# Cross-attention with experts on Trainium2: weighted sums of two steps made together, x transposed in one piece

## The reference

```python
def _L0_xattn_ref(x, y, Wq, Wkv, Wproj, bproj):
    q = (x @ Wq).reshape(b, lq, H, DK).transpose(0, 2, 1, 3)
    kv = (y @ Wkv).reshape(b, lkv, 2, H, DK).transpose(2, 0, 3, 1, 4)
    k, v = (kv[0], kv[1])
    atten = softmax(einsum('bhid,bhjd->bhij', q, k) * SCALE, axis=-1)
    res = einsum('bhij,bhjd->bhid', atten, v)
    return res.transpose(0, 2, 1, 3).reshape(b, lq, H * DK) @ Wproj + bproj
...
x = x + _L0_xattn_ref(_layernorm(x), ctx_768, Wq, Wkv, Wproj, bproj)
x = x + _L0_ffn_ref(_layernorm(x), gate_w, gate_up_w, down_w)   # top 2 of 8 experts, silu(gate) * up, down
```

## Time and profile before

| | |
|---|---|
| median of 3 runs | 1473.92 us (1473.84 to 1474.1) |
| the profiled execution | 1469.35 us, of which the span of the profile is 1467.6 |
| PE busy | 1426.4 us (97% of the span) |
| DVE busy | 1054.7 us (72%) |
| ACT busy | 854.5 us (58%) |
| POOL busy | 624.9 us (43%) |
| PE's granted clock | 0.994 of full speed over the span |
| the chain that ended last | PE 91%, DVE 3%, DMA 3% |
| W blocks in that chain (L1555) | 11%; transposes of exponentials (L1531) 10% |

### The profile page before, as it was taken

One profiled execution on the slowest core, in us unless ns is written; L12 is line 12 of the kernel. 1 busy time (PEld: TensorE's weight loads), 2 busy tenths in 40 slices (PEclk: granted clock), 3 DMA queues, 4 the chain that ended last, 5 costly groups with the idle time before them and its releaser, 6 DMA issues.

```text
span 1467.6 us, 38599 instructions
## 1 busy us (share of the span) xinstructions
PE 1426.4 (97%) x11960; PEld 1264.4 (86%) x11961; DVE 1054.7 (72%) x2868; ACT 854.5 (58%) x2392; POOL 624.9 (43%) x671
## 2 busy tenths in 40 slices
PE   6999999999999999999999999999997999999996
PEld 5888889888888888888888898888886788888885
DVE  5667777777777777777777777777767776666664
ACT  5566556555665566656655656566555565555553
POOL 3634344344545343544344444545436243333332
PEclk9999999999999999999999999999999999999999
DMA  9322222222222232322222222212128243333232
GB/s 264 108 68 69 75 72 76 67 76 67 73 67 75 72 88 76 99 74 67 73 67 77 70 73 70 73 38 73 31 64 312 50 69 54 57 51 57 51 57 26
DMA packets 101508, 114.75 MB, mean 78 GB/s; under 512 B 17276, under 2 KB 88172, under 8 KB 101356
## 3 DMA queue, kind: packets, MB, share of 16 engines
q1 hardware_dynamic: 88300, 95.25, 22.3%
q0 software_dynamic: 12144, 15.66, 6.0%
q10 hardware_dynamic: 1024, 3.34, 0.7%
HBM read 62.28 MB, written 51.93 MB: 78 GB/s over the span
## 4 chain that ended last, share of the span: by engine, by line
PE 91%; DVE 3%; DMA 3%; issue 1%; ACT 0%; ACTq 0%; POOLq 0%; DVEq 0%; SPq 0%
PE bank L1486 26%; PE bank L1429 21%; PE bank L1555 11%; PE bank L1531 10%; PE bank L1521 9%; PE bank L1576 6%; PE bank L1493 4%; DMA out<-y_out,dest_now 2%; PE bank L1729 2%; DVE probT L1285 1%; PE bank L1682 1%; DVE Wgu L1138 1%; DMA WkU_whole<-in_L_xattn_Wkv 1%; DVE stat L1127 0%; DVE x L1125 0%
## 5 line engine op out<-in xcount | busy, mean ns | idle before, releaser
L891 ACT ACTIVATE prob<-bank,neg_max 112x375 f32<-112x375 f32 x512 | 300.4, 589 | 136.1 <-DVE neg_max L1279 136.1
L1279 DVE TENSOR_REDUCE neg_max<-bank 112x1 f32<-112x375 f32 x512 | 243.8, 539 | 16.4 <-PE bank L1521 16.3
L1531 PE MATMUL bank<-ident,prob 112*125 112x112 f32 x1536 | 213.8, 273 | 2.6 <-ACT prob L891 2.4
L1531 PEld LDWEIGHTS bank<-ident,prob 112*125 112x125 f32 x1536 | 198.3, 188 | 16.1 <-ACT prob L891 4.7
L1555 PEld LDWEIGHTS bank<-probT,V 125*64 125x64 f32 x3072 | 149.0, 137 | 39.7 <-issue 37.0
L822 POOL DMA_INDIRECT out<-y_out,dest_now x63 | 97.8, 1552 | 199.9 <-DMA out<-y_out,dest_now 139.8
L1046 DVE TENSOR_TENSOR K_l<-bank,K_h 128x376 fp32r<-128x376 f32 x256 | 140.3, 549 | 57.1 <-ACT K_h L847 52.7
L1555 PE MATMUL bank<-probT,V 125*64 125x112 f32 x3072 | 176.6, 264 | 3.3 <-DVE probT L1285 2.5
L1429 PE MATMUL bank<-Wgu,hT_h 128*128 x504 | 164.7, 408 | 3.4 <-DVE hT_l L1347 2.8
L845 ACT COPY V<-bank 125x512 f32<-125x512 f32 x96 | 56.4, 587 | 164.7 <-PE bank L1493 162.2
L847 ACT CAST K_h<-bank 128x376 fp32r<-128x376 f32 x256 | 121.0, 473 | 31.2 <-PE bank L1486 29.7
(11 more groups left out here) (217 smaller groups left out, 3962.1 us busy)
## 6 DMA issues: line engine op xcount, KB each, us to landing
bins<-pad_rows SPq DMA_DIRECT2D x29, 1032.0 KB, 6.0
inv_rows<-sums SPq DMA_DIRECT2D x126, 128.0 KB, 2.9
h_in<-bins SPq DMA_DIRECT2D x63, 129.0 KB, 2.2
Wgu<-in_L_ffn_gate_up_w SPq DMA_DIRECT2D x6, 1024.0 KB, 6.8
y_sb<-in_ctx SPq DMA_DIRECT2D x32, 187.5 KB, 2.7
y_sb<-in_ctx SPq DMA_DIRECT2D x62, 93.8 KB, 2.7
x_sb<-in_x SPq DMA_DIRECT2D x16, 224.0 KB, 2.9
x_res<-in_x SPq DMA_DIRECT2D x32, 112.0 KB, 2.5
```

The lines of the kernel that those rows point to most:

```text
L891: nc.scalar.activation(prob[:, j, :], S_ps[j][0:LQ, 0:LKV], ACT.Exp, bias=neg_max[:, j:j + 1], accum_out=row_sum[:, head // HB, head % HB: ...
L1279: nc.vector.tensor_reduce(neg_max[:, j:j + 1], S_ps[j][0:LQ, 0:LKV], AX.X, ALU.max, negate=True).then_inc(max_done, 1)
L1531: last = nc.tensor.transpose(S_ps[j][0:KR, t * LQ:t * LQ + LQ], prob[:, j, t * KR:t * KR + KR], ident[0:LQ, 0:LQ])
```

## The change

The weighted sums of steps 0 and 1 are made together at the end of step 1, those of steps 2 and 3 at the end of step 3, in all pairs but the last (`merged`). For that `probT` becomes two buffers, one for even and one for odd steps. Scores of odd steps now wait for the copies of the even step's turned exponentials themselves, since `weigh` no longer stands in between. The K, V and q products stay in their steps. The four transposes of x are one item, "early" in step 3 of the even batch; q 7 moves from "mid" to "late" in step 2 of the even batch. ACT's and DVE's copies of x's transposes are one of 448 columns in place of two of 224.

The second `probT` takes the place of tables of the experts, which move to the region of `Wd`. So the first part of `Wd` is loaded not at the start of pair 14 but in the even batch of pair 15, behind the first expert's weights, and SP waits there until the weighted sums of all earlier pairs are made.

```diff
--- before.py
+++ after.py
@@ -71,12 +71,12 @@
 
 
     q_at = {(1, 0): (0,), (1, 1): (1,), (1, 2): (2, 3), (1, 3): (4,), (0, 0): (5,), (0, 1): (6,), (0, 2): (7,)}.get((odd, s), ())
-    one = [("q", p) for p in q_at] + {(0, 2): [("xT", 0)], (0, 3): [("xT", 1)]}.get((odd, s), [])
+    one = [("q", p) for p in q_at] + {(0, 3): [("xT", 0)]}.get((odd, s), [])
     places = {"K": [("K", 2 * s), ("K", 2 * s + 1)],
               "early": one if s != 2 else [],
-              "mid": one[:1] if s == 2 else [],
+              "mid": one[:-1] if s == 2 else [],
               "V": [("V", t) for t in {0: ((1, 1), (1, 2)), 1: ((0, 0), (0, 1)), 3: ((0, 2), (1, 0))}.get(s, ())],
-              "late": one[1:] if s == 2 else []}
+              "late": one[-1:] if s == 2 else []}
     return [(odd, s, place, kind, a) for place in PLACES for kind, a in places[place]]
 
 
@@ -84,7 +84,7 @@
 SECOND = ((1, 2), (0, 1), (1, 0))
 PAIR = [it for odd in (0, 1) for s in range(NS) for it in ahead(odd, s)]
 START = [(1, -1, "K", kind, a) for kind, a in (
-    ("K", 0), ("xT", 0), ("xT", 1), ("K", 1), ("K", 2), ("K", 3), ("q", 0), ("q", 1), ("K", 4), ("K", 5), ("q", 2),
+    ("K", 0), ("xT", 0), ("K", 1), ("K", 2), ("K", 3), ("q", 0), ("q", 1), ("K", 4), ("K", 5), ("q", 2),
     ("K", 6), ("K", 7), ("q", 3), ("q", 4), ("V", (0, 0)), ("V", (0, 1)), ("V", (0, 2)), ("V", (1, 0)))]
 START_BANKS = [k % 6 for k in range(len(START) - 4)] + [6, 7, 0, 1]
 LAST = [it for it in PAIR if it[3] != "xT" and not (it[0] and (it[3] in "Kq" or it[4] not in NOW))]
@@ -197,6 +197,11 @@
 def by_vector(b):
 
     return not known(b) or b < B - 3
+
+
+def merged(i):
+
+    return not known(i) or i < NP - 1
 
 
 def dram_at(t, b):
@@ -250,11 +255,7 @@
         place["at"] += 2 * 2 * 2 * FF * 4
         shared_from = place["at"]
         gw_wide = nc.alloc_sbuf_tensor_at("gw_wide", [LQ, E, C], F32, offset=wgu_at)
-        gw_rows = nc.alloc_sbuf_tensor_at("gw_rows", [LQ, C, E], F32, offset=wgu_at + E * C * 4)
-        weighed = nc.alloc_sbuf_tensor_at("weighed", [LQ, 2, C], F32, offset=wgu_at + E * C * 4)
-        multiplied = nc.alloc_sbuf_tensor_at("multiplied", [LQ, E // 2, C], F32, offset=wgu_at + E * C * 4 + 2 * C * 4)
-        logits = nc.alloc_sbuf_tensor_at("logits", [LQ, E], F32, offset=wgu_at + E * C * 4 + (2 + E // 2) * C * 4)
-        assert 2 * E * C * 4 <= shared_from - wgu_at
+        assert E * C * 4 + 4 * KT * LQ * 4 <= shared_from - wgu_at
 
 
         WqH = sb("WqH", [P, 2, HD], F32R)
@@ -269,7 +270,8 @@
         q_l = sb("q_l", [P, NJ, 2 * LQ], F32R)
         V = sb("V", [KR, KT, HD], F32)
         prob = sb("prob", [LQ, 4, LKV], F32)
-        probT = sb("probT", [KR, 4, KT * LQ], F32)
+        probT = [sb("probT", [KR, 4, KT * LQ], F32),
+                 nc.alloc_sbuf_tensor_at("probT_odd", [KR, 4, KT * LQ], F32, offset=wgu_at + E * C * 4)]
         x_sb = sb("x_sb", [LQ, 2, C], F32)
 
 
@@ -328,6 +330,12 @@
         wd_at = base + size - E * FJ * C * 4
         assert place["at"] <= wd_at
         early = 2
+        gw_rows = nc.alloc_sbuf_tensor_at("gw_rows", [LQ, C, E], F32, offset=wd_at)
+        place["at"] = wd_at
+        weighed = sb("weighed", [LQ, 2, C], F32)
+        multiplied = sb("multiplied", [LQ, E // 2, C], F32)
+        logits = sb("logits", [LQ, E], F32)
+        assert place["at"] <= wd_at + early * FJ * C * 4 and E <= early * FJ
         place["at"] = wd_at + early * FJ * C * 4
         y_sb = sb("y_sb", [P, 2, 2, LKV], F32)
         yA_h = sb("yA_h", [P, 2, LKE], F32R)
@@ -532,9 +540,6 @@
 
             def pair(i):
                 a = Ahead(i)
-                if known(i) and i == NP - 2:
-                    sp.dma_start(Wd[:, 0:early].rearrange("p e k n -> p (e k) n"),
-                                 down_w[0:early].rearrange("e (k p) n -> p (e k) n", p=P)).then_inc(wd_early, 16)
                 for odd in (0, 1):
                     b = 2 * i + odd
                     if there(b, B):
@@ -555,7 +560,10 @@
                         spread_inverses(b, 0)
                     if known(i) and i == NP - 1 and not odd:
                         sp.wait_ge(gates_done, B - 3)
+                        sp.wait_ge(pv_made, NS * (B - 2))
                         load_expert(sp, 0)
+                        sp.dma_start(Wd[:, 0:early].rearrange("p e k n -> p (e k) n"),
+                                     down_w[0:early].rearrange("e (k p) n -> p (e k) n", p=P)).then_inc(wd_early, 16)
                     if known(i) and i == NP - 1 and odd:
                         sp.dma_start(Wd[:, early:E].rearrange("p e k n -> p (e k) n"),
                                      down_w[early:E].rearrange("e (k p) n -> p (e k) n", p=P)).then_inc(wd_in, 16)
@@ -665,7 +673,7 @@
                 pool.tensor_tensor(std1[:, :, 1], std1[:, :, 0], minus_half[:, 0:2], ALU.pow).then_inc(rs1, 1)
                 if not known(pair) or pair > 0:
                     a = Ahead(pair - 2 if not known(pair) or pair > 1 else None)
-                    pool.wait_ge(made, a.made(a.find(int(a.first), "xT", 1)))
+                    pool.wait_ge(made, a.made(a.find(int(a.first), "xT", 0)))
                 pool.wait_ge(rs1, pair + 1)
                 pool.sem_inc(passed, 1)
                 for r in range(2):
@@ -848,8 +856,7 @@
                 elif kind == "q":
                     nc.scalar.copy(q_h[:, arg, :], src[:, 0:2 * LQ]).then_inc(hi_done, 1)
                 else:
-                    nc.scalar.copy(xT_h[:, :, arg * LQ:arg * LQ + LQ],
-                                   src[:, 0:2 * LQ].rearrange("p (k q) -> p k q", k=2)).then_inc(hi_done, 1)
+                    nc.scalar.copy(xT_h[:].rearrange("p k q -> p (k q)"), src[:, 0:4 * LQ]).then_inc(hi_done, 1)
 
             def hi_of_experts(first, end):
                 for e in range(first, end):
@@ -891,10 +898,10 @@
                 nc.scalar.activation(prob[:, j, :], S_ps[j][0:LQ, 0:LKV], ACT.Exp, bias=neg_max[:, j:j + 1],
                                      accum_out=row_sum[:, head // HB, head % HB:head % HB + 1]).then_inc(exp_done, 1)
 
-            def turned(b, s, j):
+            def turned(b, s, j, to):
 
                 act.wait_ge(probT_made, H * b + 4 * s + j + 1)
-                nc.scalar.copy(probT[:, j, :], S_ps[j][0:KR, 0:KT * LQ]).then_inc(probT_second, 1)
+                nc.scalar.copy(to[:, j, :], S_ps[j][0:KR, 0:KT * LQ]).then_inc(probT_second, 1)
 
             def sum_experts(b):
 
@@ -940,8 +947,9 @@
                         if s == 1 and there(b - 2, B):
                             open_gates(b - 2, logits if by_vector(b - 2) else C_ps)
                         if there(b, B):
-                            turned(b, s, 2)
-                            turned(b, s, 3)
+                            to = probT[s % 2 if merged(i) else 0]
+                            turned(b, s, 2, to)
+                            turned(b, s, 3, to)
                         if s == 0 and there(b - 2, B) and by_vector(b - 2):
                             sum_experts(b - 2)
                         for k in made_at["late"]:
@@ -1041,8 +1049,8 @@
                 elif kind == "q":
                     lo, ps, hi = q_l[:, arg, :], src[:, 0:2 * LQ], q_h[:, arg, :]
                 else:
-                    lo, hi = xT_l[:, :, arg * LQ:arg * LQ + LQ], xT_h[:, :, arg * LQ:arg * LQ + LQ]
-                    ps = src[:, 0:2 * LQ].rearrange("p (k q) -> p k q", k=2)
+                    lo, hi = [t[:].rearrange("p k q -> p (k q)") for t in (xT_l, xT_h)]
+                    ps = src[:, 0:4 * LQ]
                 nc.vector.tensor_tensor(lo, ps, hi.bitcast(F32), ALU.subtract).then_inc(lo_done, 1)
 
 
@@ -1279,10 +1287,10 @@
                 nc.vector.tensor_reduce(neg_max[:, j:j + 1], S_ps[j][0:LQ, 0:LKV],
                                         AX.X, ALU.max, negate=True).then_inc(max_done, 1)
 
-            def turned(b, s, j):
+            def turned(b, s, j, to):
 
                 dve.wait_ge(probT_made, H * b + 4 * s + j + 1)
-                nc.vector.tensor_copy(probT[:, j, :], S_ps[j][0:KR, 0:KT * LQ]).then_inc(probT_first, 1)
+                nc.vector.tensor_copy(to[:, j, :], S_ps[j][0:KR, 0:KT * LQ]).then_inc(probT_first, 1)
 
             def pair(i):
                 a = Ahead(i) if there(i, NP) else None
@@ -1304,12 +1312,13 @@
                             normalise(b, 0)
                         if s == 2 and there(b - 1, B):
                             residual(i, b - 1, 1 - odd, A_ps[1])
+                        to = probT[s % 2 if merged(i) else 0]
                         if there(b, B):
-                            turned(b, s, 0)
+                            turned(b, s, 0, to)
                         for k in made_at["early"]:
                             low_part(a, k)
                         if there(b, B):
-                            turned(b, s, 1)
+                            turned(b, s, 1, to)
                         for k in made_at["mid"]:
                             low_part(a, k)
```

(24 more changed lines are left out.)

## The result

The changed kernel takes 1497.8 us (median of 6 runs, 1495.98 to 1500.69) where the kernel before takes 1474.01 (6 runs beside it, 1472.93 to 1476.83). The ratio is 1.016, with a 95% interval of 1.0149 to 1.0172: slower by 1.6%. The forecast was 1493, slower. The profiled execution took 1498.88 us, its span 1497.1. That is 29.5 more than the span before, 6 more than the medians differ. Some 2.9 of it is the load at the start: the first scores stand at 33.74 for 30.81, and this start lay anywhere from 29.8 to 33.7 in the profiles of this study. The rest is the loop: 14 pairs at 70.96 for 69.03 are 27.0.

A forecast was written before the change was run, and what follows sets the result against it. PE, busy 199.86 of 200 us in the loop, was taken as the bound. 2 x 0.34 + 0.56 + 0.15 = 1.39 us a pair, 19.5 over pairs 1 to 14, on 1473.9 gave 1493 us; 8 in 10: 1470 to 1501.

The forecast's parts named there:

- The price of W: Block of weighted sums on PE: a second block behind the first costs 1.13 us instead of 1.30, saving 0.17 a merge.
- Place A: Step 0 to step 1, twice a pair: K tails wait for ACT's V copy to free bank 0; +0.34 us each.
- the restart: At Place A: ACT's copy ends at 624.10, PE waits until 624.14; restarting after a wait costs another 0.10 us.
- nothing behind 623.80 would wait: Place A, forward from 623.80: no further wait over 0.05 us was found.
- Place B: Step 2 to 3, even batch, once a pair: scores wait for q 7's low part, only 0.78 us earlier; +0.56 us.
- ACT's wider copy: Step 3, even batch: ACT's copy of x, twice as wide, delays the last exponential by some 0.2 us.
- Place C: Step 2 to 3, odd batch, once a pair: V product about 1.0 us earlier, not 1.30; +0.15 us.
- the 0.45 for ACT's wait: Place C: ACT no longer has a wait for K among the exponentials, taken as 0.45 us.
- PE's 0.15 in hand: Place C: PE has some 0.15 us in hand behind the last of the exponentials.
- Covered but for q 7: Rival: A and C lose nothing, only q 7's wait costs; +0.08 us a pair, 1475 us; chance 0.10.
- faster: Rival: all waits hidden, ACT frees bank 0 0.40 us earlier; -0.95 us a pair, 1461 us; chance 0.16.
- Worse: Rival: A's wait delays K's product, exponentials and transposes in turn; A costs 0.8 us, 1505 us; chance 0.12.

## Why the prediction was right, and where it was off

**The road of thought held.** PE's row sets the end, W costs 1.13 in a double block, and cover is lost in places A, B and C: each stands in the trace after, with the releaser that the forecast named. A pair came out 1.93 longer against 1.39.

**The price of W** was sized well. Forecast 1.13 for the second block, 0.17 saved; measured 1.15 and 0.15. The way from the last V product to the tails without W is 0.32 (605.00 to 605.32, scores at 605.65) where rows 5 gave 0.33.

**Place A** was the right mechanism, 0.09 too small each time: forecast +0.34. Measured were +0.63 (odd) and +0.48 (even), and with the scatter left out steps 0 and 1 take 17.08 in both batches, for 16.66 and 16.64 before: +0.42 and +0.44. The term that was mis-sized is the restart. I had set 0.04 from the end of ACT's copy to PE's start; it is 0.13 in all 28 (642.60 to 642.74 in the rounded row), and the K tails stand 0.48 later against the scores. Moving the sums gave back 0.58, so all that follows the stop, the slow restart among it, is 0.1. The claim that nothing behind 623.80 would wait is borne out: V is the only releaser in PE's waits there.

**Place B:** forecast +0.56, measured +0.69. The scores are 0.63 earlier, not 0.78, 0.08 for the same reason (0.12 from q's low part to PE, 695.27 to 695.39, and not 0.04), and 0.06 because the twelve transposes take 1.22 to q 7 (692.32 to 693.54) and not two times 0.58. The second block of W costs 0.02 more than forecast. Step 3 was read rightly: x's two further transposes fill a wait that was there, and ACT's wider copy, forecast at 0.2, makes the step 0.18 longer, with the moves alone and in the whole change.

**Place C:** forecast +0.15, measured +0.13. The V product comes 1.15 - 0.13 = 1.02 earlier, and 1.0 was the value taken between the bounds of 0.42 and 1.30. That it came out so close is luck in part: the 0.45 for ACT's wait and PE's 0.15 in hand were taken from no row, and the K tails' wait for `running`, 0.14, was not in the forecast. Cutting the assignment gave back 0.29, with the K tails at 1.12 again, which shows that DVE was the cause.

**What was missing** is the scatter: 0.29 a pair by the kernel without it, 4 us. POOL's indirect DMAs lay 2.17 and 0.80 ahead of the V tails in the kernel before (613.18 and 614.55 to 615.35) and delayed nothing; the moved steps brought them to 2.87 and 1.27, and there they did. The forecast counted each engine's queue forward but took the wait for PE's signal as fixed.

**The sum:** 0.86 + 0.69 + 0.13 for the three places are 1.68, with 0.21 and 0.04 by which the scatter lengthens the two steps 0 it is 1.93, as measured by the pair. Over 14 pairs the forecast is short by 7.6: 14 x 0.29 = 4.1 from the places and 14 x 0.25 = 3.5 from the scatter. That 1493 lies only 4.8 below the median is luck for the rest: the profiled executions differ by 29.5 and the medians by 23.8, since the one before lay 4.7 below its median and the one after 1.1 above. Beyond the 2.9 of the start it isn't settled where that comes from.

**The rivals.** "Covered but for q 7" and "faster" needed ACT to free bank 0 by the time of the K tails: it was 0.3 late in all 28 cases counted. "Worse", by waits that feed each other, needed 0.8 at A and found 0.43. By the Trainium skill (TensorE: Matmul & The Clock Gate, Part 2: What happens when you issue a matmul), from whose drain of about 128 cycles the prediction estimated 0.05 for a switch, and hence a merge worth 0.05, the second block would cost 1.25; the trace has 1.15, so it speaks for the rows.
